# Two data-dependent blurs: inverse squares one row further ahead, and another split of the images between VectorE and GpSimd

## The chip, the cores and the metric

The program runs on one core of a Trainium2 chip. The metric is the device time in microseconds of one execution, lower is better. TensorE does the matrix products and transposes, VectorE (DVE), ScalarE (ACT) and GpSimd (POOL) the elementwise work, and SyncE (SP) starts transfers. Each engine works through its own instructions in the order in which the program lists them, and waits on semaphores for the others.

## What is computed

Eight images of 16 channels and 64 x 64 pixels pass through four layers, all in float32: L0 (a normalisation, depthwise convolutions and attention), L1 (a blur), L2 (a binary 3 x 3 convolution) and L3 (a blur again, with other weights). The change touches only the two blurs. Cut to what matters, a blur is:

```python
h = relu(einsum('bchw,co->bohw', x, w1) + b1)              # 32 hidden channels
ks = relu(einsum('bohw,o->bhw', h, w2[:, 0]) + b2[0]) * 20.0 + 1.0
sigma = ks / 3.0                                           # one width for each pixel
logits = -gauss_kernel / (2.0 * sigma[..., None, None] ** 2)   # 9 x 9 taps
wgt = exp(logits)
wgt = wgt / sum(wgt, axis=(-2, -1))
# low_freq = sum over the 81 taps of shifted x times wgt
enhanced = x + low_freq
out = (enhanced - mean) / sqrt(var + 1e-05)                # over h, w of each channel
```

The exponent of a tap is thus a fixed number (-4.5 times a squared distance) times 1/ks^2 of the pixel. This text calls these 1/ks^2 the inverse squares.

## The kernel before, in words

`blur` treats the picture in RB = 8 rows of blocks (r = 0 to 7), each of 8 pixel rows for all eight images. For a row r:

- **Inverse squares.** TensorE computes the hidden layer (`pe_hidden`, L921) and the sum over it (`pe_ks`, L930); ScalarE applies the activation between the two (`act_hidden`, L1040). VectorE adds the bias and clips (`dve_relu`, L1091), ScalarE squares (`act_square`, L1048), VectorE takes the reciprocal into `srow` (`dve_inverse`, L1099). From `srow` there are two ways. For the images that VectorE multiplies, TensorE turns it (`pe_ks_turn`, L937), VectorE copies it to `scl` (`dve_scale`, L1105), and TensorE spreads it over the partitions into one of four PSUM banks, four transposes for an image (`pe_spread`, L960). For the images that GpSimd multiplies, SyncE writes `srow` to DRAM (L1241) and reads it back broadcast to all partitions as `s_wide` (L1247).
- **Exponents.** VectorE multiplies the exponents by the inverse squares of an image (`dve_logit`, L1115), GpSimd does the same for its images (`pool_logit`, L1202). ScalarE takes the exponential of two images (a pair) at a time (`act_weight`, L1067). Pair k holds images 2k and 2k+1. The weights are in `wgt[r % 2]`.
- **Pixels.** GpSimd stages the row's pixels (`pool_stage`, L1190), TensorE transposes them (`pe_xt`, L945), ScalarE copies them to `xt` (`act_xt`, L1055).
- **Blur.** TensorE multiplies weights and pixels (`pe_blur`, L974), for images 0 to 3 (i = 0) and 4 to 7 (i = 1), each in two parts. VectorE copies each half's sum out of the one bank O_BANK (`dve_num`, L1123). TensorE turns it (`pe_turn`, L988), VectorE divides by the sum of the weights (`dve_mix`, L1129 and L1133), TensorE turns it back (`pe_low`, L996), and VectorE adds it to the picture and takes statistics (`dve_enhance`, L1141, `dve_stats`, L1145).

The work of several rows is interleaved, and the order on each engine is written out by hand in `pe_row`, `act_row`, `dve_row` and `pool_row`. In the pass of row r, TensorE ends row r-1's images 4 to 7, blurs row r's images 0 to 3, spreads row r+1 and computes the hidden layer of row r+2; VectorE prepares row r+1's inverse squares while it multiplies row r. `rows_of` writes out rows 0 and 1 and 6 to 8, and runs rows 2 to 5 in a hardware loop of two turns. Row 0 has all eight images on VectorE. Waits are on counts: `small` counts relu, reciprocal and scale, three a row; `logit` the images of VectorE; `logit_p` those of GpSimd; `weight` the exponentials; `blurred` the half blurs.

VectorE's order in a middle row of the kernel before, as `dve_row` has it: relu(r+1), image 0 of row r, inverse(r+1), image 1, scale(r+1), mix and num of row r-1, images 2 and 3 of its four, mix(r-1), num(r, 0), enhance(r-1), stats(r-1). The names of its four images are 0, 1, 4 and 5. ScalarE's order: square(r+1), the exponentials of pair 1 (GpSimd's images 2, 3), pair 0, the xt copy of row r+1, pair 3 (GpSimd's 6, 7), the hidden activations of row r+2, pair 2.

Of the kernel before, what the change touches and what calls it, by code (L numbers as in the profile page):

```python
# [836 lines left out]
def blur(nc, sem_, sb, tag, later, ident, vec, ps, pad, norm, to_clear, out, beside=None):  # L837
# [62 lines left out]
    def is0(r):  # L900
        return isinstance(r, int) and r == 0

    def slots(r):

        return list(enumerate(range(B) if is0(r) else BY_DVE))

    def by_slot(r, v):

        return v + 1 if is0(r) else 4 * r + 5 + v
# [148 lines left out]
    def act_weight(act, r, s, pair):  # L1058

        if is0(r):  # L1060
            act.wait_ge(logit, 2 * pair + 2)
        elif pair % 2 == 0:
            act.wait_ge(logit, by_slot(r, pair + 1))
        else:
            act.wait_ge(logit_p, 4 * r + pair - 5 + 2)
# [3 lines left out]
    def act_row(act, r, s, do):  # L1069
        if do.next and not do.first:  # L1070
            act_square(act, r + 1)
        if do.main:
            act_weight(act, r, s, 0 if do.first else 1)
        if do.next and do.first:
            act_square(act, r + 1)
        if do.main:
            act_weight(act, r, s, 1 if do.first else 0)
            act_xt(act, r + 1, 1 - s)
            act_weight(act, r, s, 2 if do.first else 3)
        if do.after_next:  # L1080
            act_hidden(act, r + 2)
        if do.main:
            act_weight(act, r, s, 3 if do.first else 2)
# [527 lines left out]
```

## Time and profile before

| | us |
|---|---|
| median of 3 runs | 533.4 |
| lowest and highest of them | 532.68, 534.13 |
| the profiled execution's own time | 531.34 |
| its span, first to last instruction | 529.4 |
| busy in the span: TensorE, VectorE, ScalarE, GpSimd | 412.6, 339.3, 260.6, 187.9 |
| the first blur lies at | 214 to 346 |
| the second blur lies at | 388.3 to 529.4 |
| mean granted TensorE clock, as a share of the full one | 0.927 |

The profile is one execution. Times in its rows are microseconds from the start of the span; L974 is line 974 of the kernel. PE is TensorE's matrix work and PEld its weight loads, which overlap. PEclk is the granted clock as a share of the full 2.4 GHz. In a timeline, a row may stand for several instructions of one kind (x8); the bracket at its end gives how long the engine was idle before it and who ended that. A row's duration can reach up to 0.1 us into the next one's start, since instructions of one engine overlap a little at their ends.

### The profile page before, as it was taken

How to read it: one execution, taken by the hardware profiler on the slowest of the kernel's cores; microseconds unless marked ns; L12 is line 12 of the kernel's file. 1: busy time of each engine (PE TensorE's matmuls, PEld its weight loads, DVE VectorE, ACT ScalarE, POOL GpSimd, SP SyncE). 2: the span in 40 equal slices, each digit the busy share in tenths (PEclk: the TensorE clock that was granted, in tenths of full speed). 3: DMA queues.
4: the chain of work that ended last, by engine and by line, in shares of the span. 5: the costliest groups of instructions: out<-in, count | busy, mean ns of one | idle time of the engine just before them, and what ended most of it. 6: DMA issues, size and time to landing. Idle time of an engine off the chain costs nothing. (4 is left out here: it accounts for less than half of the span.)

```text
span 529.4 us, 16123 instructions
## 1 busy us (share of the span) xinstructions
PE 412.6 (78%) x7024; PEld 293.8 (56%) x7024; DVE 339.3 (64%) x525; ACT 260.6 (49%) x284; POOL 187.9 (35%) x132
## 2 busy tenths in 40 slices
PE   4588998877999469668888888579956888788780
PEld 2277942225988412436666667457734666566660
DVE  2694587753888964554666668539534576566863
ACT  0664476663333000147767776511015577677771
POOL 3320013220000000307777777500030567867740
PEclk9968999996999869789999999979988899999986
DMA  8830000000000000002222223000000222222203
GB/s 190 194 136 1 2 1 0 1 0 1 4 2 1 3 0 0 1 6 79 83 84 81 80 82 84 2 1 1 0 1 0 83 85 83 84 80 80 83 4 158
DMA packets 17046, 24.67 MB, mean 47 GB/s; under 512 B 6736, under 2 KB 8545, under 8 KB 16865
## 3 DMA queue, kind: packets, MB, share of 16 engines
q1 hardware_dynamic: 15968, 23.52, 15.0%
q8 instruction: 43, 0.70, 0.5%
q10 hardware_dynamic: 1024, 0.36, 0.4%
q14 instruction: 11, 0.08, 0.0%
HBM read 21.53 MB, written 2.34 MB: 45 GB/s over the span
## 5 line engine op out<-in xcount | busy, mean ns | idle before, releaser
L1202 POOL TENSOR_TENSOR g_wgt<-g_exponents,g_s_wide 128x1024 f32<-128x1024 f32 x56 | 131.4, 2382 | 67.9 <-DMA g_s_wide<-g_s_rows 67.9
L1067 ACT ACTIVATE g_wgt<-g_wgt 128x2048 f32<-128x2048 f32 x64 | 121.6, 1909 | 17.2 <-DVE g_wgt L1115 11.0
L974 PE MATMUL ps<-g_wgt,g_xt 128*32 128x64 f32 x4096 | 72.5, 222 | 29.2 <-ACT g_wgt L1067 13.1
L974 PEld LDWEIGHTS ps<-g_wgt,g_xt 128*32 128x32 f32 x4096 | 62.0, 111 | 49.3 <-issue 36.9
L1115 DVE TENSOR_TENSOR g_wgt<-g_exponents,ps 128x1024 f32<-128x1024 f32 x72 | 84.6, 1202 | 2.6 <-PE ps L960 2.6
L1123 DVE COPY g_num<-ps 128x512 f32<-128x512 f32 x32 | 22.0, 687 | 64.0 <-PE ps L974 63.9
L1040 ACT ACTIVATE g_hid<-ps,vec 128x512 f32<-128x512 f32 x32 | 20.2, 683 | 84.0 <-PE ps L921 84.0
L960 PE MATMUL ps<-ident,g_scl 128*128 128x128 f32 x288 | 46.8, 302 | 4.9 <-DVE g_wgt L1115 2.6
L960 PEld LDWEIGHTS ps<-ident,g_scl 128*128 128x128 f32 x288 | 34.7, 150 | 10.4 <-DVE g_wgt L1115 4.2
L469 PE MATMUL ps<-conv_img,projblk 128*32 128x512 f32 x256 | 35.8, 679 | 0.0
L1412 PE MATMUL ps<-high,wb 128*128 128x512 f32 x72 | 30.3, 421 | 5.3 <-DVE rest L1441 5.3
L1190 POOL COPY g_tile<-pad_a 128x512 f32<-128x512 f32 (+1 forms) x18 | 10.6, 620 | 60.9 <-POOLq L732 53.4
L1055 ACT COPY g_xt<-ps 128x1024 f32<-128x1024 f32 x18 | 18.2, 1010 | 27.8 <-PE ps L945 27.8
L1190 POOL COPY g_tile<-pad_b 128x512 f32<-128x512 f32 (+1 forms) x18 | 10.6, 626 | 58.7 <-POOLq L1401 50.6
L526 ACT ACTIVATE biased<-ps,beta_o 128x512 f32<-128x512 f32 x32 | 24.0, 771 | 13.2 <-PE ps L469 13.2
L1412 PE MATMUL ps<-rest,wb 128*128 128x512 f32 x72 | 30.0, 416 | 0.0
L666 ACT ACTIVATE e<-ps 128x512 f32<-128x512 f32 x16 | 9.6, 597 | 33.0 <-PE ps L628 33.0
L787 PE MATMUL ps<-xrow,outblk 128*64 128x512 f32 x32 | 16.2, 1086 | 11.9 <-DVE xcol L827 11.9
L469 PEld LDWEIGHTS ps<-conv_img,projblk 128*32 128x32 f32 x256 | 12.5, 112 | 20.6 <-issue 16.1
L945 PE MATMUL ps<-ident,g_tile 128*128 128x128 f32 x144 | 22.1, 304 | 0.0
L988 PE MATMUL ps<-ident,g_num 128*128 128x128 f32 x128 | 20.3, 281 | 1.9 <-DVE g_num L1123 1.9
L617 PE MATMUL ps<-ident,rnh 128*128 128x128 f32 x128 | 19.1, 297 | 2.3 <-POOL rnh L709 2.3
(165 smaller groups left out, 718.0 us busy)
## 6 DMA issues: line engine op xcount, KB each, us to landing
g_s_wide<-g_s_rows SPq DMA_DIRECT2D x56, 256.0 KB, 3.8
x<-in_x SPq DMA_DIRECT2D x8, 256.0 KB, 6.8
x<-in_x SPq DMA_DIRECT2D x1, 2048.0 KB, 8.4
out<-g_result SPq DMA_DIRECT2D x4, 512.0 KB, 3.9
windows<-band SPq DMA_DIRECT2D x4, 256.0 KB, 5.1
g_s_rows<-g_srow SPq DMA_DIRECT2D x56, 4.0 KB
c_weight<-in_c_weight SPq DMA_DIRECT2D x1, 576.0 KB, 3.9
g_w<-in_g_w SPq DMA_DIRECT2D x2, 128.0 KB, 2.7
```

Source lines behind the costliest of these rows:

```text
L469: mm = pe.matmul(ps[q:q + 32, j % 4, :], projblk[:, 64 * cp + 32 * late:64 * cp + 32 * late + 32], lines(t, inner, strip, side), start=Tru ...
L526: act.activation(biased[:, j % 4, :], ps[:, j % 4, :], ACT.Identity, bias=beta[:, t:t + 1], scale=1.0).then_inc(proj_biased, 1)
L945: tr = pe.transpose(ps[:, bank, P * (cb % 4):P * (cb % 4) + P], tile[s][:, cb].rearrange("p r c -> p (r c)"), ident[:])
L960: tr = pe.transpose(ps[:, v % 4, P * k:P * k + P], spread(scl[s][:, k, b:b + 1], [P, P]), ident[:])
L974: mm = pe.matmul(ps[32 * j:32 * j + 32, O_BANK, 64 * cb:64 * cb + 64], xt[(s + t) % 2][:, cb, b, :], weights_of(s, b)[:, t, cb, :], start= ...
L988: tr = pe.transpose(ps[:, NT_BANK, P * k:P * k + P], num[i][:, P * k:P * k + P], ident[:])
L1067: act.activation(w, w, ACT.Exp).then_inc(weight, 1)
L1115: dve.tensor_tensor(weights_of(s, b), spread(gband[:].unsqueeze(2), shape), spread(s_in_ps, shape), ALU.mult).then_inc(logit, 1)
L1123: dve.tensor_copy(num[i][:], ps[:, O_BANK, :]).then_inc(num_out, 1)
L1190: ins = pool.tensor_copy(tile[s][:].rearrange("p (k o) r c -> p o k r c", o=2)[:, odd], cols.rearrange("p r (k c) -> p k r c", c=QC))
L1202: pool.tensor_tensor(weights_of(s, b), spread(gband[:].unsqueeze(2), shape), spread(s_wide[s][j][:].unsqueeze(1), shape), ALU.mult).then_i ...
L1412: mm = pe.matmul(ps[:, g % 4, :], wb[:, t, :], part[:, ROWS * g + dh:ROWS * g + dh + ROWS, dw:dw + W], start=(k == 0), stop=(k == 2 * TAPS ...
```

## The change

- Inverse squares are prepared for row r+2 in the pass of row r (relu, square, reciprocal, turn, scale, and SyncE's two transfers with them), where it was row r+1; the hidden layer and its sum for row r+3, where it was r+2. `scl` gets a third buffer. The place of these instructions among their neighbours in `pe_row` and `dve_row` stays.
- GpSimd multiplies images 3, 6 and 7 of a row, VectorE images 0, 1, 2, 4 and 5. TensorE spreads five images of a row, the fifth in the row's own pass, between the turn and the second part of the half blur. The banks now go by a running number (`nth`).
- ScalarE takes the exponentials in the order of pairs 0, 1, 2, 3, with the xt copy behind pair 1. Pair 1 now has one image of each engine.
- Half of the staging of pixels from row 2 on moves from GpSimd to ScalarE (`act_stage`, counted by `staged_a`), behind the xt copy.
- Rows 2 to 5 are written out, without the hardware loop. Row 0's pass has a function of its own for each engine, in which the inverse squares of rows 1 and 2 and the hidden layers of rows 2 and 3 are computed.

```diff
-    scl = [sb(f"scl{s}", [P, 4, B]) for s in range(2)]
+    scl = [sb(f"scl{s}", [P, 4, B]) for s in range(3)]
...
-    BY_DVE, BY_POOL = (0, 1, 4, 5), (2, 3, 6, 7)
+    BY_DVE, BY_POOL = (0, 1, 2, 4, 5), (3, 6, 7)
...
+    def image(r, v):
+        return v if r == 0 else BY_DVE[v]
+    def nth(r, v):
+        return v if r == 0 else B + len(BY_DVE) * (r - 1) + v
...
-        pe.wait_ge(small, 3 * RB if isinstance(g, int) and g == RB else 3 * g + 3)
+        if g >= 2:
+            pe.wait_ge(staged_a, g - 1)
+        pe.wait_ge(small, 3 * g + 3 if g < 2 else min(3 * g + 6, 3 * RB))
...
+    def pe_first_row(pe):
+        pe_spread(pe, 0, 0, 4)
+        pe_spread(pe, 0, 0, 5)
+        pe_ks_turn(pe, 1, 1)
+        pe_spread(pe, 0, 0, 6)
+        pe_spread(pe, 0, 0, 7)
+        pe_xt(pe, 1, 1)
+        pe_hidden(pe, 2)
+        pe_ks(pe, 2)
+        pe_spread(pe, 1, 1, 0)
+        pe_spread(pe, 1, 1, 1)
+        pe_ks_turn(pe, 2, 0)
+        pe_blur(pe, 0, 0, 0, 0)
+        pe_spread(pe, 1, 1, 2)
+        pe_hidden(pe, 3)
+        pe_blur(pe, 0, 0, 0, 1)
+        pe_spread(pe, 1, 1, 3)
+        pe_ks(pe, 3)
+    def pe_row(pe, r, s):
+        pe_blur(pe, r - 1, 1 - s, 1, 0)
+        pe_turn(pe, r - 1, 0)
+        if r + 2 < RB:
+            pe_ks_turn(pe, r + 2, s)
+        if r < RB:
+            pe_spread(pe, r, s, 4)
+        pe_blur(pe, r - 1, 1 - s, 1, 1)
+        if r + 1 < RB:
             pe_spread(pe, r + 1, 1 - s, 0)
             pe_spread(pe, r + 1, 1 - s, 1)
-        if do.main:
+        if r < RB:
             pe_xt(pe, r + 1, 1 - s)
-        if do.lag:
-            pe_turn(pe, r - 1, 1)
-        if do.main:
+        pe_turn(pe, r - 1, 1)
+        if r < RB:
             pe_blur(pe, r, s, 0, 0)
-        if do.next:
+        if r + 1 < RB:
             pe_spread(pe, r + 1, 1 - s, 2)
-        if do.after_next:
-            pe_hidden(pe, r + 2)
-        if do.main:
+        if r + 3 < RB:
+            pe_hidden(pe, r + 3)
+        if r < RB:
             pe_blur(pe, r, s, 0, 1)
-        if do.lag:
-            pe_low(pe, r - 1)
-        if do.next:
+        pe_low(pe, r - 1)
+        if r + 1 < RB:
             pe_spread(pe, r + 1, 1 - s, 3)
-        if do.after_next:
-            pe_ks(pe, r + 2)
+        if r + 3 < RB:
+            pe_ks(pe, r + 3)
...
+    def act_stage(act, g, s):
+        act.wait_ge(xt_mm, g - 1)
+        act.copy(*half_tile(g, s, 1)).then_inc(staged_a, 1)
+    def act_first_row(act):
+        act_weight(act, 0, 0, 0)
+        act_square(act, 1)
+        act_weight(act, 0, 0, 1)
+        act_xt(act, 1, 1)
+        act_stage(act, 2, 0)
+        act_hidden(act, 2)
+        act_square(act, 2)
+        act_weight(act, 0, 0, 2)
+        act_hidden(act, 3)
+        act_weight(act, 0, 0, 3)
+    def act_row(act, r, s):
+        if r + 2 < RB:
+            act_square(act, r + 2)
+        act_weight(act, r, s, 0)
+        act_weight(act, r, s, 1)
+        act_xt(act, r + 1, 1 - s)
+        if r + 2 <= RB:
+            act_stage(act, r + 2, s)
+        act_weight(act, r, s, 2)
+        if r + 3 < RB:
+            act_hidden(act, r + 3)
+        act_weight(act, r, s, 3)
...
+    def dve_first_row(dve):
+        dve_logit(dve, 0, 0, 0)
+        dve_logit(dve, 0, 0, 1)
+        dve_relu(dve, 1)
+        dve_logit(dve, 0, 0, 2)
+        dve_inverse(dve, 1, 1)
+        dve_logit(dve, 0, 0, 3)
+        dve_scale(dve, 1, 1)
+        dve_logit(dve, 0, 0, 4)
+        dve_relu(dve, 2)
+        dve_logit(dve, 0, 0, 5)
+        dve_inverse(dve, 2, 0)
+        dve_logit(dve, 0, 0, 6)
+        dve_scale(dve, 2, 0)
+        dve_logit(dve, 0, 0, 7)
+        dve_num(dve, 0, 0)
+    def dve_row(dve, r, s):
+        if r + 2 < RB:
+            dve_relu(dve, r + 2)
+        if r < RB:
             dve_logit(dve, r, s, 0)
-        if do.next:
-            dve_inverse(dve, r + 1, 1 - s)
-        if do.main:
+        if r + 2 < RB:
+            dve_inverse(dve, r + 2, s)
+        if r < RB:
             dve_logit(dve, r, s, 1)
-        if do.next:
-            dve_scale(dve, r + 1, 1 - s)
+        if r + 2 < RB:
+            dve_scale(dve, r + 2, s)
+        if r < RB:
+            dve_logit(dve, r, s, 2)
         dve_mix(dve, r - 1, 0)
         dve_num(dve, r - 1, 1)
-        if do.main:
-            dve_logit(dve, r, s, 2)
+        if r < RB:
             dve_logit(dve, r, s, 3)
+            dve_logit(dve, r, s, 4)
         dve_mix(dve, r - 1, 1)
...
+    def half_tile(g, s, odd):
+        cols = pad[:, BLK * g:BLK * g + BLK, BLK * odd:BLK * odd + W]
+        return (tile[s][:].rearrange("p (k o) r c -> p o k r c", o=2)[:, odd],
+                cols.rearrange("p r (k c) -> p k r c", c=QC))
     def pool_stage(pool, g, s):
-        if not (isinstance(g, int) and g < 2):
+        if g >= 2:
             pool.wait_ge(xt_mm, g - 1)
-        for odd in range(2):
-            cols = pad[:, bass.ds(BLK * g, BLK), BLK * odd:BLK * odd + W]
-            ins = pool.tensor_copy(tile[s][:].rearrange("p (k o) r c -> p o k r c", o=2)[:, odd],
-                                   cols.rearrange("p r (k c) -> p k r c", c=QC))
-        ins.then_inc(staged, 1)
+        else:
+            pool.tensor_copy(*half_tile(g, s, 1))
+        pool.tensor_copy(*half_tile(g, s, 0)).then_inc(staged, 1)
...
+    def pool_row(pool, r, s):
+        for j in range(len(BY_POOL)):
+            pool_logit(pool, r, s, j)
+        if r + 2 <= RB:
             pool_stage(pool, r + 2, s)
...
-    def rows_of(eng, row):
-        for r in range(2):
-            row(eng, r, r, Row(r))
-        with eng.Fori(0, 2) as i:
-            for p in range(2):
-                row(eng, 2 * i + 2 + p, p, Row(2))
-        for r in range(RB - 2, RB + 1):
-            row(eng, r, r % 2, Row(r))
...
-            rows_of(pool, pool_row)
+            pool_stage(pool, 2, 0)
+            for r in range(1, RB):
+                pool_row(pool, r, r % 2)
```

## Rows read from the trace of the kernel before

**Rows 1.** Windows: us, busy us (x instructions) by engine, PEclk, DMA share, GB/s
```profile
245.51:257.96 12.45, 10.77 (x310) 8.35 (x310) 8.24 (x13) 9.89 (x9) 8.66 (x7) 1.00 0.29 88
257.96:299.49 41.53, 34.51 (x941) 26.49 (x942) 28.52 (x45) 30.11 (x25) 31.81 (x19) 1.00 0.28 79
299.49:313.15 13.66, 11.41 (x315) 8.78 (x314) 9.46 (x16) 10.01 (x9) 10.51 (x7) 1.00 0.27 79
313.15:324.77 11.62, 9.59 (x310) 8.04 (x309) 9.45 (x15) 9.92 (x8) 8.44 (x6) 1.00 0.34 90
324.77:339.92 15.15, 10.88 (x416) 9.00 (x416) 10.93 (x17) 10.36 (x7) 12.92 (x5) 1.00 0.03 7
...
432.64:475.02 42.38, 34.50 (x941) 26.48 (x941) 28.38 (x45) 30.09 (x25) 32.17 (x20) 1.00 0.24 78
...
500.31:516.16 15.85, 12.51 (x416) 10.50 (x415) 11.13 (x18) 10.34 (x7) 8.32 (x4) 0.89 0.02 4
```

**Rows 2.** Timeline of VectorE: start us, us, engine, line, operation, [idle before, releaser]
```profile
324.77 0.69 DVE L1123 COPY g_num<-ps 128x512 f32<-128x512 f32 x1 [1.96 <-PE ps L974]
...
326.71 2.34 DVE L1115 TENSOR_TENSOR g_wgt<-g_exponents,ps 128x1024 f32<-128x1024 f32 x2
...
446.15 0.69 DVE L1123 COPY g_num<-ps 128x512 f32<-128x512 f32 x1 [3.98 <-PE ps L974]
...
448.49 1.21 DVE L1115 TENSOR_TENSOR g_wgt<-g_exponents,ps 128x1024 f32<-128x1024 f32 x1
```

**Rows 3.** Timeline of ScalarE, block 7 of the first blur, block 3 of the second
```profile
328.70 3.71 ACT L1067 ACTIVATE g_wgt<-g_wgt 128x2048 f32<-128x2048 f32 x2 [3.19 <-POOL g_wgt L1202]
332.31 0.99 ACT L1055 COPY g_xt<-ps 128x1024 f32<-128x1024 f32 x1
...
448.91 1.90 ACT L1067 ACTIVATE g_wgt<-g_wgt 128x2048 f32<-128x2048 f32 x1
451.67 1.91 ACT L1067 ACTIVATE g_wgt<-g_wgt 128x2048 f32<-128x2048 f32 x1 [0.86 <-DVE g_wgt L1115]
453.98 1.01 ACT L1055 COPY g_xt<-ps 128x1024 f32<-128x1024 f32 x1 [0.39 <-PE ps L945]
```

**Rows 4.** Timeline of TensorE in block 3 of the second blur
```profile
450.61 0.33 PE L937 MATMUL ps<-ident,g_srow 128*128 128x128 f32 x1 [0.73 <-DVE g_srow L1099]
...
455.23 1.10 PE L974 MATMUL ps<-g_wgt,g_xt 128*32 128x64 f32 x64 [0.93 <-ACT g_xt L1055]
456.26 0.65 PE L960 MATMUL ps<-ident,g_scl 128*128 128x128 f32 x4
456.75 1.88 PE L921 MATMUL ps<-pad_b,g_w 128*128 x4
```

**Rows 5.** Waits, whole span: us in total, times, longest us
```profile
POOL g_wgt L1202 <- DMA g_s_wide<-g_s_rows: 67.9, 14, 13.8
```

**Rows 6.** Timelines of row 0 in both blurs, then one window of it
```profile
233.70 0.94 DVE L1099 RECIPROCAL g_srow<-g_ks_sq 128x128 f32<-128x128 f32 x1
...
241.01 1.10 PE L974 MATMUL ps<-g_wgt,g_xt 128*32 128x64 f32 x64 [1.19 <-ACT g_xt L1055]
...
401.74 1.98 PE L921 MATMUL ps<-pad_b,g_w 128*128 128x512 f32 x4 [1.10 <-ACT g_xt L1055]
...
405.79 0.35 DVE L1091 TENSOR_SCALAR g_relu<-ps,vec 128x128 f32<-128x128 f32 x1 [6.94 <-PE ps L930]
...
408.57 0.95 DVE L1099 RECIPROCAL g_srow<-g_ks_sq 128x128 f32<-128x128 f32 x1 [0.17 <-ACT g_ks_sq L1048]
...
410.76 2.24 PE L960 MATMUL ps<-ident,g_scl 128*128 128x128 f32 x8 [0.84 <-DVE g_scl L1105]
...
412.80 1.70 PE L945 MATMUL ps<-ident,g_tile 128*128 128x128 f32 x8
...
409.50:412.80 3.30, 2.36 (x10) 1.77 (x11) 3.30 (x5) 0.85 (x1) 0.00 (x0) 0.69 0.03 8
```

More of the change, by code:

```diff
@@ L900, in is0 @@
     def is0(r):
[L901 to L909, printed above, removed]
+        return r == 0
+    def image(r, v):
+        return v if r == 0 else BY_DVE[v]
+    def nth(r, v):
+        return v if r == 0 else B + len(BY_DVE) * (r - 1) + v
     def weights_of(s, b):
@@ L915, in pe_hidden @@
     def pe_hidden(pe, r):
-        if not is0(r):
+        if r == 1 or r == 2:
             pe.wait_ge(xt_out, r)
-        rows = bass.ds(BLK * r + R, BLK)
+        elif r > 2:
+            pe.wait_ge(xt_out, r - 1)
+            pe.wait_ge(small, 3 * r)
+        rows = slice(BLK * r + R, BLK * r + R + BLK)
         for i, bank in enumerate((MLP_BANK, XT_BANK)):
@@ L1058, in act_weight @@
     def act_weight(act, r, s, pair):
[L1060 to L1065, printed above, removed]
+        on_dve = [v for v in range(B if r == 0 else len(BY_DVE)) if image(r, v) // 2 == pair]
+        on_pool = [j for j, b in enumerate(BY_POOL) if r > 0 and b // 2 == pair]
+        if on_dve:
+            act.wait_ge(logit, nth(r, on_dve[-1]) + 1)
+        if on_pool:
+            act.wait_ge(logit_p, len(BY_POOL) * (r - 1) + on_pool[-1] + 1)
         w = wgt[s][pair][:].rearrange("p b t k m -> p (b t k m)")
         act.activation(w, w, ACT.Exp).then_inc(weight, 1)
-    def act_row(act, r, s, do):
-        if do.next and not do.first:
-            act_square(act, r + 1)
-        if do.main:
-            act_weight(act, r, s, 0 if do.first else 1)
-        if do.next and do.first:
-            act_square(act, r + 1)
-        if do.main:
[L1077 to L1083, printed above, removed]
+    def act_stage(act, g, s):
[24 more added lines that the diff above has]
+        act_weight(act, r, s, 3)
     def dve_relu(dve, r):
@@ L1096, in dve_inverse @@
         dve.wait_ge(ks_squared, r + 1)
-        if not (isinstance(r, int) and r < 3):
+        if not (r < 3):
             dve.wait_ge(s_stored, 64 * (r - 2))
@@ L1203, in pool_logit @@
                            spread(s_wide[s][j][:].unsqueeze(1), shape), ALU.mult).then_inc(logit_p, 1)
-    def pool_row(pool, r, s, do):
-        if do.main and not do.first:
-            for j in range(len(BY_POOL)):
-                pool_logit(pool, r, s, j)
-        if do.next:
-            pool_stage(pool, r + 2, s)
-    class Row:
-        def __init__(self, r):
-            self.first, self.main, self.lag = r == 0, r < RB, 0 < r <= RB
-            self.next, self.after_next = r + 1 < RB, r + 2 < RB
-    def rows_of(eng, row):
-        for r in range(2):
-            row(eng, r, r, Row(r))
-        with eng.Fori(0, 2) as i:
-            for p in range(2):
-                row(eng, 2 * i + 2 + p, p, Row(2))
-        for r in range(RB - 2, RB + 1):
-            row(eng, r, r % 2, Row(r))
+    def pool_row(pool, r, s):
+        for j in range(len(BY_POOL)):
+            pool_logit(pool, r, s, j)
+        if r + 2 <= RB:
+            pool_stage(pool, r + 2, s)
     def quarter(j):
@@ L1281, in _ @@
             pe.wait_ge(const_ready, 4)
-            rows_of(pe, pe_row)
+            pe_first_row(pe)
+            for r in range(1, RB + 1):
+                pe_row(pe, r, r % 2)
         @block.scalar
@@ L1290, in _ @@
             act_hidden(act, 1)
-            rows_of(act, act_row)
+            act_first_row(act)
+            for r in range(1, RB):
+                act_row(act, r, r % 2)
             act.wait_ge(tail, 2)
@@ L1316, in _ @@
             dve.wait_ge(band_ready, 2)
-            rows_of(dve, dve_row)
+            dve_first_row(dve)
+            for r in range(1, RB + 1):
+                dve_row(dve, r, r % 2)
             dve.wait_ge(stat, RB)
```

69 lines of the change are left out of this document (18 added, 51 removed).

## Prediction

> **What bounds the kernel now.** I read the windows of the two blurs first. The change touches only these; they fill 214 to 346 and 388 to 529 us of the span. A window here runs from one start of the copy at L1123 to the next, that is from one image row block r to the following one. I call this start num(r). In both blurs a middle block lasts 13.66 us, the first 12.45, the sixth 11.6; the last stretch holds the block of row 7 and the remainder up to the second copy [rows 1]. No engine fills a middle block: TensorE is busy 11.4 of 13.66, VectorE 9.5, ScalarE 10.0, GpSimd 10.5. So a chain through several engines sets it, and its links count, not the sums.
>
> The timelines give the links. From num(2) at 446.15 VectorE runs copy, enhance, statistics, relu, the first image of the next block (448.49), the reciprocal of the inverse squares, and the second image [rows 2]. That second image releases the exponential of pair 0 at 451.67, 5.52 us after num. ScalarE has by then done the exponential of pair 1, GpSimd's pair, at 448.91, in time that it would otherwise idle away. Then it idles 0.86 and, after pair 0, 0.39 us, the latter for TensorE's staging transposes, and copies xt at 453.98 [rows 3]. TensorE waits for that copy (0.93) and runs half blur, spread, hidden layer, half blur; their end is the next num [rows 4]. TensorE's own arm of the loop (turn at 450.61, which waits 0.73 for the reciprocal, half blur, two spreads, transposes) reaches xt at the same time as ScalarE's arm, to 0.4 us. GpSimd is a side arm: it waits 67.9 us in all for the broadcast rows, 14 times, but its result is late only where ScalarE shows a wait on it, in row 7 of a blur (3.19 us in the first) [rows 5, 3].
>
> **The change, part by part.**
>
> *Order of pairs.* In the new row order ScalarE does square, exp of pair 0, exp of pair 1, xt copy. The exp of pair 0 still needs the second image of the row, which in VectorE's order still stands behind num, enhance, statistics, relu, image 0 and the reciprocal; only the index of relu and reciprocal has grown. So pair 0 starts as late as before, and pair 1 can't fill the wait, because it is behind it. Two exponentials back to back put the xt copy 3.61 us after the first one's start (328.70 to 332.31), where it was 2.31 us (451.67 to 453.98) [rows 3]. **+1.30 us for each block**, on the path.
>
> *One more spread and image.* VectorE gets a fifth image, GpSimd loses one. An image costs VectorE 1.17 us (two in 2.34) [rows 2]. In VectorE's order image 2 falls behind image 1, which is released already; it ends near num+6.6, image 4 near num+10.2. Cover: VectorE idles 3.98 us ahead of num and pair 2's exponential starts near num+10.5. Zero on the path; without the cover 1.2 a block. TensorE gets four transposes, between the turn and the half blur: 0.55 us, the size of one spread (0.49 in steps, 0.65 as shown) [rows 4]. Its arm then reaches the end of the xt transposes near num+8.2 (7.7 before), while ScalarE is now free only at num+9.0. So this spread is hidden behind the exponential; without this cover, 0.55 a block.
>
> *GpSimd.* Three images of 2.38 us and half a staging copy instead of four and a whole one. Its inputs come a row earlier, and its idle time grows. Off the path: worth nothing in middle blocks. In row 7 it ends the wait of 3.19 us, but there the exponentials now wait for VectorE's images: 324.77 to 326.71 is 1.94, two images 2.34, so they start at num+4.3 where GpSimd let them start at 328.70, num+3.9 [rows 2, 3].
>
> *ScalarE's half staging copy.* No such copy exists there; between 0.5 us (half the xt copy, which is twice as large and takes 1.01 [rows 3]) and 1.0; I take 0.6. It stands behind the xt copy, which is the last thing of ScalarE that TensorE waits for, and ScalarE is idle for 3.6 of 13.66 us. Zero.
>
> *Loops unrolled.* Between num and image 0 the unrolled row needs 1.94 us where the loop row needs 2.34, with a relu of 0.26 (0.35 as shown, 0.09 under the next): 0.14 saved. Blocks 5 and 6 differ by 2.04, the hidden layer is 1.81 of it (1.88 as shown); the other 0.23 is what the loop costs elsewhere [rows 1, 2, 4, 6]. **−0.37 in blocks 2 to 5.** One gap of 1.3 us in the second blur's loop, which TensorE spends on issue, makes its blocks 2 to 4 last 42.38, not 41.53; I take it to be gone.
>
> *The first row.* Before, VectorE ran images 0 to 7 of row 0 with one relu and reciprocal between. Now it has relu(2) between images 4 and 5. relu(2) waits for a whole chain: image 3 (now behind reciprocal(1)), spread 7, transposes, xt copy, hidden(2), activation, ks(2). Images 5, 6, 7 are queued behind that wait, and so are the exponentials of pairs 2 and 3 and the second reciprocal; TensorE has this turn ahead of its first half blur. From reciprocal(1) on, by the second blur: reciprocal and image 0.95 + 1.17, spread 1.12 (two in 2.24), transposes 1.70, xt copy 1.01, hidden to relu 4.05 (401.74 to 405.79), relu and image 0.35 + 1.17, reciprocal 0.95, turn 0.3, less some 0.2 by which they overlap: 12.6 us to the first half blur. Before it was 415.69 − 408.57 = 7.12. **+5.4.** In the first blur the reciprocal can start one image (1.17) earlier than its 233.70, and the old way took 241.01 − 233.70 = 7.31: 12.6 − 1.17 − 7.31 = **+4.1** [rows 6]. From the half blur to num(0) the work is the same, 4.5 us (241.01 to 245.51).
>
> The clock enters here. The granted clock was 0.69 from 409.5 to 412.8, after TensorE had waited several times, and 1.00 in all middle blocks; eight spread transposes took 2.24, where four take 0.65 in a middle block [rows 6, 1, 4]. The new first row leaves TensorE with more waits, so I take the slow values. The Trainium skill (TensorE: Matmul & The Clock Gate, "What's actually happening") says that the full clock is released by activity and the default is half of it; by it a head that stays at full clock would be some 1.1 us shorter in each blur (0.5 in the spread, 0.6 in the transposes), 2.2 in all. The trace agrees so far as these rows go.
>
> **The sum.** New blocks: row 1 has no loop, and its xt copy waits as the others do: 12.45 + 1.3 = 13.75. Rows 2 to 4: 13.66 + 1.30 − 0.37 = 14.6 each. Row 5 loses the hidden layer: 14.6 − 1.88 = 12.7. Row 6 has neither relu nor reciprocal: first exponential at num+4.3, xt 3.61 later, and from there 3.9 to the next num (11.62 − 5.38 − 2.31): 11.8. Row 7 and the remainder: xt at num+7.95, and from xt to the second copy 339.92 − 332.31 = 7.6: 15.55. Together 13.75 + 43.8 + 12.7 + 11.8 + 15.55 = 97.6. Before: first blur 12.45 + 41.53 + 13.66 + 11.62 + 15.15 = 94.4; second 12.45 + 42.38 + 13.66 + 11.63 + 15.85 = 96.0 (its blocks 1, 5 and 6 agree with the first's to 0.01) [rows 1]. So +3.2 and +1.6, and the heads +4.1 and +5.4: **+14.3 us**. The profiled execution took 531.34 us with a span of 529.4 and lies 2.1 below the median of 533.4. On the median: **548 us**, 2.8% slower.
>
> **Rivals.**
> 1. *Only TensorE's arm counts.* The exponential of pair 1 would not push xt, or my 1.30 is given back by another link. For it: the two arms were only 0.4 us apart. Against it: ScalarE's order is fixed. Then a block grows by 0.55 and not 1.30, 0.75 less in 14 blocks, 10.5 us less: 537. Chance 0.08.
> 2. *Faster: the reciprocal's place was the bound.* If taking it a row ahead truly takes TensorE's turn off the row's loop, each block gives back the 0.73 wait, 12 blocks, the loop costs 0.37 in 8, and GpSimd's lateness about 3 in each row 7: 8.8 + 3.0 + 6 = 18 less, against heads of 9.5: 525. It decides from the point where a block is shorter than about 13.0. Against it: relu, reciprocal and turn keep their places between the same neighbours in all three queues. Chance 0.06.
> 3. *The clock drops in the rows.* TensorE now idles 2 to 3 us a block in pieces; if the granted clock fell as in the heads, five spreads at 0.9 or more instead of 0.55 and the rest alike would add some 3 us a block, on 14 blocks 42 on top: 590. Nothing shows a fall in middle blocks, where idle pieces of 0.9 us are already borne at 1.00. Part of it, in the heads and row 7 (0.89 in the last stretch [rows 1]), is more likely and adds 2 to 5: up to 553. Chance of the first 0.03.
> 4. *The change does nothing that can be told:* its losses meet gains of the same size, within 0.3%, which is 1.6 us and about what a measurement of this kernel can tell from no change: 533. Chance 0.03.
>
> **How the numbers follow.** My forecast has 0.80, with its own range of 543 to 553 (heads 1.5 either way each, staging and spread up to 0.2 a block). The range for 8 in 10 takes in rival 1 below and the clock's part above: 537 to 554. Faster holds rival 2 and a remainder, 0.08; same 0.03; slower 0.89.
>
> **What would show it.** In the new profile: middle blocks of 14.6 us at clock 1.00; two exponentials back to back ahead of each xt copy, ScalarE idle 2.5 us ahead of them; no ScalarE wait on GpSimd, and GpSimd below 60% in the blurs; TensorE's wait for xt near 1.7 us; in the first row a wait of some 6 us of VectorE at relu for TensorE. Blocks under 13.7 or a first row as short as before would prove me wrong.

## The result, and the profile after

The changed kernel takes 552.6 us, median of 4 runs (551.83 to 554.7); the kernel of before took 533.07 beside it, median of 4. The ratio is 1.0369, with a 95% interval of 1.0337 to 1.0402: 19.5 us slower. The forecast was 548, with a range of 537 to 554. The profiled execution has a span of 550.1 us against 529.4. Here and below a median is over all runs of a kernel, while a ratio is over the undisturbed runs of both kernels of one session, so that quotients of medians differ a little from the ratios.

The windows of the changed kernel, cut as those of [rows 1] at the starts of the first copy of a row (blocks 1, 2 to 4, 5, 6, and 7 with the remainder; the second blur's blocks 1, 5 and 6 read 13.82, 12.85 and 11.79):

```profile
248.22:262.04 13.82, 11.34 (x314) 8.71 (x314) 9.38 (x15) 10.30 (x10) 7.64 (x4) 1.00 0.30 83
262.04:305.85 43.81, 36.04 (x952) 27.57 (x952) 31.69 (x49) 31.23 (x28) 22.93 (x12) 1.00 0.18 58
305.85:320.16 14.31, 10.48 (x314) 8.56 (x314) 10.56 (x16) 11.14 (x9) 7.65 (x4) 1.00 0.21 59
320.16:331.95 11.79, 9.58 (x297) 8.01 (x298) 9.40 (x13) 7.49 (x6) 9.18 (x4) 1.00 0.02 4
331.95:347.42 15.47, 11.31 (x420) 9.28 (x420) 12.07 (x18) 10.87 (x7) 2.29 (x1) 1.00 0.01 3
...
449.75:493.49 43.74, 35.94 (x952) 27.46 (x952) 31.69 (x49) 31.24 (x28) 22.94 (x12) 1.00 0.19 58
...
518.13:536.80 18.67, 14.52 (x420) 11.63 (x420) 12.16 (x18) 10.86 (x7) 0.00 (x0) 0.82 0.01 3
```

A middle block now lasts 14.6 us (43.81 and 43.74 for three) where it took 13.66. All of them have a granted clock of 1.00, so nothing here comes from a slower TensorE. The last stretch of the second blur has 0.82. The same links as in [rows 2 to 4], in block 3 of the second blur, first on VectorE:

```profile
449.75 0.69 DVE L1155 COPY g_num<-ps 128x512 f32<-128x512 f32 x1 [3.91 <-PE ps L977]
...
451.93 1.21 DVE L1147 TENSOR_TENSOR g_wgt<-g_exponents,ps 128x1024 f32<-128x1024 f32 x1
453.06 0.94 DVE L1131 RECIPROCAL g_srow<-g_ks_sq 128x128 f32<-128x128 f32 x1
453.92 1.16 DVE L1147 TENSOR_TENSOR g_wgt<-g_exponents,ps 128x1024 f32<-128x1024 f32 x1
...
455.09 1.21 DVE L1147 TENSOR_TENSOR g_wgt<-g_exponents,ps 128x1024 f32<-128x1024 f32 x1
```

then on ScalarE:

```profile
455.11 3.73 ACT L1085 ACTIVATE g_wgt<-g_wgt 128x2048 f32<-128x2048 f32 x2 [2.67 <-DVE g_wgt L1147]
458.75 0.98 ACT L1073 COPY g_xt<-ps 128x1024 f32<-128x1024 f32 x1
459.64 0.61 ACT L1090 COPY g_tile<-pad_b 128x512 f32<-128x512 f32 x1
```

and on TensorE (turn, the fifth image's spread, first half blur):

```profile
454.06 0.33 PE L941 MATMUL ps<-ident,g_srow 128*128 128x128 f32 x1 [0.56 <-DVE g_srow L1131]
454.22 0.60 PE L963 MATMUL ps<-ident,g_scl 128*128 128x128 f32 x4
...
459.83 1.10 PE L977 MATMUL ps<-g_wgt,g_xt 128*32 128x64 f32 x64 [1.51 <-ACT g_wgt L1085]
```

From num at 449.75 the exponential of pair 0 starts 5.36 us later (5.52 before, with the loop). Image 2 on VectorE starts at 455.09, the exponential of pair 1 follows that of pair 0 at once (3.73 for both), and the xt copy comes 3.64 us after the start of the first; in [rows 3] it was 2.31. TensorE waits 1.51 us for it, where it waited 0.93 [rows 4]. (The bracket names the exponential, but that had ended at 458.84; the matmuls wait for both and start 0.1 us after the copy's end.) ScalarE idles 2.67 us ahead of the exponentials. Who waited for whom, over the whole span:

```profile
POOL g_wgt L1244 <- PE ps L977: 69.2, 22, 3.7
...
ACT g_wgt L1085 <- DVE g_wgt L1147: 45.3, 18, 4.5
...
DVE g_relu L1123 <- PE ps L934: 33.3, 8, 8.3
...
PE ps L977 <- ACT g_wgt L1085: 29.8, 28, 1.7
```

GpSimd no longer waits mainly for the broadcast rows [rows 5] but for the half blurs that free its weights: its inputs come early, and it is 27% busy where it was 35%. No wait of ScalarE for GpSimd is left. All that was bought is slack on an engine that wasn't setting the pace, but for its lateness in row 7. The new first row, one line of the first blur and then the second blur, with two windows of it:

```profile
240.13 0.35 DVE L1123 TENSOR_SCALAR g_relu<-ps,vec 128x128 f32<-128x128 f32 x1 [5.74 <-PE ps L934]
...
417.18 1.16 DVE L1147 TENSOR_TENSOR g_wgt<-g_exponents,ps 128x1024 f32<-128x1024 f32 x1
...
418.35 1.21 DVE L1147 TENSOR_TENSOR g_wgt<-g_exponents,ps 128x1024 f32<-128x1024 f32 x1
...
419.02 1.91 PE L951 MATMUL ps<-ident,g_tile 128*128 128x128 f32 x8
...
422.04 3.71 PE L925 MATMUL ps<-pad_b,g_w 128*128 128x512 f32 x4 [1.10 <-ACT g_xt L1073]
...
427.82 0.35 DVE L1123 TENSOR_SCALAR g_relu<-ps,vec 128x128 f32<-128x128 f32 x1 [8.26 <-PE ps L934]
...
430.62 1.91 PE L977 MATMUL ps<-g_wgt,g_xt 128*32 128x64 f32 x64
...
418.50:421.00 2.50, 2.44 (x12) 2.04 (x12) 1.06 (x1) 1.81 (x2) 0.00 (x0) 0.54 0.09 32
422.00:425.80 3.80, 3.71 (x4) 1.17 (x4) 0.00 (x0) 0.52 (x2) 2.28 (x1) 0.53 0.43 130
```

VectorE waits 5.74 us for relu(2) in the first blur and 8.26 in the second. There TensorE works at half its clock (0.54 and 0.53, thus 1.2 GHz): the hidden layer takes 3.71 us where 1.98 and 1.88 are seen in [rows 6, 4], the half blur 1.91 instead of 1.10.

### The profile page after: what moved, and what is told of

Read it like the earlier page. It is cut to its first block and busy times, and to the rows that moved or that the text cites. A ratio compares the mean times of both kernels' runs of the same rounds, so it can differ in the third digit from the quotient of the medians.

```text
span 550.1 us, 15973 instructions
## 1 busy us (share of the span) xinstructions
PE 422.2 (77%) x7080; PEld 299.3 (54%) x7080; DVE 356.2 (65%) x539; ACT 267.2 (49%) x298; POOL 148.7 (27%) x104
## 5 line engine op out<-in xcount | busy, mean ns | idle before, releaser
L1085 ACT ACTIVATE g_wgt<-g_wgt 128x2048 f32<-128x2048 f32 x64 | 120.1, 1907 | 45.3 <-DVE g_wgt L1147 45.3
L1244 POOL TENSOR_TENSOR g_wgt<-g_exponents,g_s_wide 128x1024 f32<-128x1024 f32 x42 | 99.1, 2376 | 105.7 <-PE ps L977 69.2
L1147 DVE TENSOR_TENSOR g_wgt<-g_exponents,ps 128x1024 f32<-128x1024 f32 x86 | 101.5, 1204 | 2.6 <-PE ps L963 2.6
L977 PE MATMUL ps<-g_wgt,g_xt 128*32 128x64 f32 x4096 | 74.6, 226 | 32.4 <-ACT g_wgt L1085 29.8
L977 PEld LDWEIGHTS ps<-g_wgt,g_xt 128*32 128x32 f32 x4096 | 63.9, 114 | 51.4 <-ACT g_wgt L1085 36.4
L963 PE MATMUL ps<-ident,g_scl 128*128 128x128 f32 x344 | 56.8, 298 | 4.4 <-DVE g_wgt L1147 3.9
L963 PEld LDWEIGHTS ps<-ident,g_scl 128*128 128x128 f32 x344 | 40.5, 147 | 12.5 <-DVE g_wgt L1147 7.9
L1123 DVE TENSOR_SCALAR g_relu<-ps,vec 128x128 f32<-128x128 f32 x16 | 5.5, 342 | 33.3 <-PE ps L934 33.3
L1073 ACT COPY g_xt<-ps 128x1024 f32<-128x1024 f32 x18 | 17.9, 994 | 14.8 <-PE ps L951 14.8
L925 PE MATMUL ps<-pad_b,g_w 128*128 128x512 f32 x32 | 17.1, 660 | 4.1 <-ACT g_xt L1073 2.2
```

Of the source, the lines that this page charges most:

```text
L963: tr = pe.transpose(ps[:, nth(r, v) % 4, P * k:P * k + P], spread(scl[r % 3][:, k, b:b + 1], [P, P]), ident[:])
L977: mm = pe.matmul(ps[32 * j:32 * j + 32, O_BANK, 64 * cb:64 * cb + 64], xt[(s + t) % 2][:, cb, b, :], weights_of(s, b)[:, t, cb, :], start= ...
L1085: act.activation(w, w, ACT.Exp).then_inc(weight, 1)
L1147: dve.tensor_tensor(weights_of(s, b), spread(gband[:].unsqueeze(2), shape), spread(s_in_ps, shape), ALU.mult).then_inc(logit, 1)
L1244: pool.tensor_tensor(weights_of(s, b), spread(gband[:].unsqueeze(2), shape), spread(s_wide[s][j][:].unsqueeze(1), shape), ALU.mult).then_i ...
```

## The experiments

All ratios are to the kernel of before, run beside each on the same chip. The blocks are the seven stretches from num(r) to num(r+1) of a blur; "middle block" gives the length of one without a gap in the first blur, "first row" the time from the first relu to the first num in the first and second blur. A "gap" is idle time of TensorE inside a run of matmuls that the profile puts down to issue, since it shows nothing that the engine waited for.

```
kernel                 median us  ratio (95%)              first row     middle block
before                 533.07     1                        27.5, 27.5    13.66
changed                552.6      1.0369 (1.0337, 1.0402)  31.3, 35.5    14.58
e1_split               540.9      1.0126 (1.0055, 1.0197)  31.9, 32.6    13.78
e2_split_spread        542.44     1.0167 (1.0104, 1.0231)  33.0, 32.6    13.78
e3_before_natural      561.16     1.0527 (1.0460, 1.0593)  27.2, 28.9    15.0, 16.5
e4_before_unrolled     531.66     0.9977 (0.9941, 1.0014)  27.5, 27.6    13.21
e5_one_ahead           531.8      1.0014 (0.9968, 1.0060)  27.4, 27.7    13.78
e6_ahead_alone         537.0      1.0087 (1.0054, 1.0119)  31.8, 35.5    13.21
e7_late_turn           533.59     0.9989 (0.9954, 1.0023)  33.0, 33.7    12.87
e8_late_turn_head      532.17     0.9998 (0.9958, 1.0038)  25.9, 26.9    12.86
e9_xt_first            529.14     0.9928 (0.9898, 0.9959)  23.5, 23.6    13.3
e10_xt_first_unrolled  527.53     0.9925 (0.9891, 0.9960)  25.9, 26.0    12.95
e11_split_natural      552.23     1.0383 (1.0321, 1.0445)  30.6, 35.5    14.57
e12_warm               542.96     1.0204 (1.0149, 1.0259)  30.6, 33.0    14.58
```

### The order of the exponentials

e1, from the changed kernel:

```diff
-    BY_DVE, BY_POOL = (0, 1, 2, 4, 5), (3, 6, 7)
+    BY_DVE, BY_POOL = (0, 1, 4, 5, 7), (2, 3, 6)
     # act_row
-        act_weight(act, r, s, 0)
         act_weight(act, r, s, 1)
+        act_weight(act, r, s, 0)
```

> The changed kernel with GpSimd on images 2, 3, 6 (VectorE 0, 1, 4, 5, 7) and the exponential of pair 1 ahead of pair 0 again. Theory (natural order puts one exponential on the path, 1.30 us a block): that exponential goes back into ScalarE's wait; then TensorE's arm sets the xt copy (near num+8.2), so middle blocks go from 14.58 to 13.8 and the last two lose about 0.95: 541 us. Rival (the exponential is all there is, TensorE's extra spread costs nothing even now): 13.3 a block, 535. Rival (order of pairs costs nothing, the extra VectorE image or the unrolled code does): 552 as before this edit.

e11 has the first of these two edits alone.

> The changed kernel with the other split alone (GpSimd 2, 3, 6, VectorE 0, 1, 4, 5, 7), exponentials in natural order. It parts the two edits of e1. Theory (the order puts the exponential on the path, whoever multiplies the images): blocks of 14.6 and about 552, 3.7% over the kernel of before. Rival (it was image 2 on VectorE that held pair 1 back): blocks of 13.8, near e1's 1.3%.

e3 is the same question asked of the kernel of before:

```diff
     # act_row, rows from 1 on
-            act_weight(act, r, s, 1)
             act_weight(act, r, s, 0)
+            act_weight(act, r, s, 1)
             act_xt(act, r + 1, 1 - s)
```

> The kernel of before with one edit: the exponential of pair 0 ahead of pair 1, ahead of the xt copy. Theory: +1.30 us in blocks 1 to 6 and +0.4 in block 7 of both blurs, 16 us more: 549.5; middle blocks 14.96. Rival (TensorE's arm sets the block, so the order is hidden): 533, blocks 13.66.

e1 takes 2.4% off the changed kernel's ratio, 13 us of the 19.5, and its blocks are 13.78; e11, with the same split but the natural order, stays at 14.57 and 3.8%. So it is the order, not who multiplies image 2. (In the changed kernel the two go together: with image 2 on VectorE, ready only after image 1, pair 1 can't come first.) Not all of the 13 us is the order, though. The profiles' blocks with the remainder are 4.2 and 6.2 us shorter in e1, and the second blur's first row is 2.9 shorter, although its code is the same in both: its hidden layer took 1.98 us in e1 and 3.71 in the changed kernel. That part is TensorE's clock. ScalarE in block 2 of e1's second blur:

```profile
445.54 1.90 ACT L1085 ACTIVATE g_wgt<-g_wgt 128x2048 f32<-128x2048 f32 x1
448.30 1.91 ACT L1085 ACTIVATE g_wgt<-g_wgt 128x2048 f32<-128x2048 f32 x1 [0.86 <-DVE g_wgt L1147]
451.10 1.01 ACT L1073 COPY g_xt<-ps 128x1024 f32<-128x1024 f32 x1 [0.89 <-PE ps L951]
```

Pair 1's exponential stands ahead, and the xt copy starts 2.8 us after pair 0's and no longer 3.64; the 0.89 idle ahead of it says that TensorE's arm sets it now. e3 went further than the forecast: +5.3% and not +3.1%. Block 4 with 15.0 us is what was expected, but others last 16.5. TensorE and the xt copy in one of these, and its window beside that of block 4:

```profile
268.04 0.99 ACT L1055 COPY g_xt<-ps 128x1024 f32<-128x1024 f32 x1
...
269.27 1.33 PE L974 MATMUL ps<-g_wgt,g_xt 128*32 128x64 f32 x64 [2.22 <-ACT g_xt L1055]
...
270.54 1.11 PE L960 MATMUL ps<-ident,g_scl 128*128 128x128 f32 x4
...
271.45 2.86 PE L921 MATMUL ps<-pad_a,g_w 128*128 x4
...
259.06:275.49 16.43, 13.12 (x315) 9.85 (x315) 9.43 (x15) 9.97 (x9) 10.32 (x7) 0.90 0.24 68
292.20:307.20 15.00, 11.40 (x316) 8.77 (x315) 9.52 (x16) 9.88 (x10) 8.77 (x6) 1.00 0.25 72
```

The granted clock is 0.90 in the long block and 1.00 in the other. TensorE had waited 2.22 us for the xt copy, and then the spread took 1.11, the hidden layer 2.86, the half blur 1.33 (0.65, 1.88 and 1.10 in [rows 4]). This is my third rival, at work in some blocks of a kernel where the wait is 2.22 and not in the changed one, where it is 1.51; its price is 1.5 us a block, half of what I gave it. Block 4 has the same wait of 2.22 and the full clock, and it idled longer ahead of the turn (0.69 against 0.39), so the wait alone doesn't decide it, and no limit is read from this.

### TensorE's arm, the fifth spread and the loop

e2, from e1:

```diff
     # pe_row
+        if r < RB:
+            pe_spread(pe, r, s, 4)
         if r + 2 < RB:
             pe_ks_turn(pe, r + 2, s)
-        if r < RB:
-            pe_spread(pe, r, s, 4)
```

> As e1, and TensorE spreads the fifth image ahead of the turn of the inverse squares, where it waits for the reciprocal anyway. Theory: the 0.55 us of the spread leaves the arm, blocks 13.3, about 5 us less than e1: 536. Rival (the spread was already covered in e1): same as e1.

> The kernel of before with rows 2 to 5 written out. Theory: 0.37 us less in each of 8 blocks: 530, blocks 13.3. Rival (loop overhead is hidden, or the longer code costs more instruction fetch): 533 or above.

e5, from e4, in short (all waits recounted):

```diff
-    BY_DVE, BY_POOL = (0, 1, 4, 5), (2, 3, 6, 7)
+    BY_DVE, BY_POOL = (0, 1, 4, 5, 7), (2, 3, 6)
     # five spreads and images a row; pairs 1, 0, xt, 2, hidden, 3
```

> Rows written out, inverse squares only one row ahead and the old first row, GpSimd on three images (2, 3, 6), the exponential of pair 1 ahead of pair 0. Against e1 this undoes the second row of look-ahead. Theory: the first row is as long as before (27.5 us from the first relu to the first copy, not 32), but the rows 5 to 7 get their old length back, since the hidden layer and the reciprocal are in them again; blocks stay at 13.8 by the fifth spread: 533. Rival (the long first row is a pure loss of some 5 us a blur): 10 us under e1, 531 or less, with rows 5 to 7 as short as in e1.

e2 brought nothing; my theory for it was wrong. TensorE in a block of e2:

```profile
451.90 0.65 PE L963 MATMUL ps<-ident,g_scl 128*128 128x128 f32 x4
452.91 0.65 PE L963 MATMUL ps<-ident,g_scl 128*128 128x128 f32 x4 [0.36 <-DVE g_wgt L1147]
```

The second spread of the next row waits 0.36 us for VectorE. The bank that it writes is free only when image 4 (VectorE's third) is multiplied. With four images to a row it was free after the second, since the four banks go round. So there is a third arm, as long as TensorE's own.

In e4 the blocks fell about as forecast (13.21, by 0.45 for 0.37), but the time by only 0.2%, which is no difference. The profile puts 13.8 us of TensorE's idle time ahead of L974 down to issue, where the kernel of before has 6.3, but 8.5 of these are 12 waits of 0.71 like this one:

```profile
263.55 1.01 ACT L1055 COPY g_xt<-ps 128x1024 f32<-128x1024 f32 x1 [0.31 <-PE ps L945]
...
264.66 1.10 PE L974 MATMUL ps<-g_wgt,g_xt 128*32 128x64 f32 x64 [0.71 <-issue]
```

The matmuls start 0.1 us after the xt copy ends, as in every one of the 12: this is the known wait for xt under another name. True gaps, in the middle of a half blur, add up to 5.2 us in e4, the longest 3.2, and to 3.5 in the kernel of before (2.8 of its 6.3 are waits for xt); 1.9 more lie among e4's transposes. That is 3.6 us more than before, as much as eight shorter blocks save. Block 6 of the first blur, with the gap of 3.2, lasts 14.9 instead of 11.6.

e5 comes to 531.8 us, near both forecasts, but its rows are the theory's: the first row is 4.5 to 4.9 us shorter than e1's in each blur, and blocks 5 to 7 are longer again, 37.5 us in the first blur where e1 has 34.9, although a gap of 2.3 us lies in these.

### The look-ahead alone, and put to use

e6, from the changed kernel, in short:

```diff
-    BY_DVE, BY_POOL = (0, 1, 2, 4, 5), (3, 6, 7)
+    BY_DVE, BY_POOL = (0, 1, 4, 5), (2, 3, 6, 7)
     # four spreads and images a row; pairs 1, 0, xt, 3, hidden, 2
```

> The look-ahead alone: two rows ahead with the new first row, rows written out, half the staging on ScalarE, but GpSimd on its four images, four spreads, and the exponentials in the old order. Theory: middle blocks of 13.2 as in the unrolled kernel of before, first row 32 us, rows 5 to 7 shorter by the work that is already done and by GpSimd's wait: 527 to 531. Rival (the first row's loss is not returned): 539.

e7, from e6:

```diff
     # pe_row
-        if r + 2 < RB:
-            pe_ks_turn(pe, r + 2, s)
         pe_blur(pe, r - 1, 1 - s, 1, 1)
         if r + 1 < RB:
             pe_spread(pe, r + 1, 1 - s, 0)
-            pe_spread(pe, r + 1, 1 - s, 1)
+        if r + 2 < RB:
+            pe_ks_turn(pe, r + 2, s)
         if r < RB:
             pe_xt(pe, r + 1, 1 - s)
+        if r + 1 < RB:
+            pe_spread(pe, r + 1, 1 - s, 1)
     # dve_row
-        if r + 2 < RB:
-            dve_inverse(dve, r + 2, s)
         if r < RB:
             dve_logit(dve, r, s, 1)
+        if r + 2 < RB:
+            dve_inverse(dve, r + 2, s)
```

> e6 with the look-ahead put to use: VectorE takes the second image ahead of the reciprocal, and TensorE turns the inverse squares only after the half blur and one spread. Theory (the reciprocal's place between num and the second image is what the row waits for): exponential of pair 0 at num+4.5 and not 5.4, xt at num+6.9, blocks of 12.5: 520. Rival (TensorE's own work sets the row by now, 11.2 us and its waits): blocks of 13.0 or more, 526 or above.

> e7 with a first row in which VectorE multiplies all eight images and copies the first sum before relu(2), and a second row that holds the second preparation. Theory (the first row is long because images 5 to 7 stand behind relu(2)): first row about 25.5 us, block 1 about 15.5, together 3 us less than e7 in each blur: 514. Rival (the chain of the preparations is serial wherever it stands): as e7.

The look-ahead alone costs 0.9% over the kernel of before (4.6 us), between the two theories: middle blocks are 13.2, the first row 31.8 and 35.5, and what the last rows give back is partly eaten by gaps (7.8 us in its half blurs and 2.0 elsewhere; another 9.2 that the profile puts down to issue are waits for xt, as in e4).

e7 shows where the look-ahead would have a use: with the reciprocal behind the second image and the turn behind the half blur, a block falls to 12.87, 0.4 above my 12.5, since the scale copy (VectorE waits 0.42 for the turn) is late. But the first row takes 33 us, and the sum is that of before. e8's first row is short (25.9), its second 19.6 and 20.7 us: the rival holds, the second preparation is a serial chain and only moved.

### The best version

e9, from the kernel of before, with neither look-ahead nor another split:

```diff
     # pe_row
-        if do.next:
-            pe_ks_turn(pe, r + 1, 1 - s)
         if do.lag:
             pe_blur(pe, r - 1, 1 - s, 1, 1)
         if do.next:
-            pe_spread(pe, r + 1, 1 - s, 0)
-            pe_spread(pe, r + 1, 1 - s, 1)
+            pe_ks_turn(pe, r + 1, 1 - s)
         if do.main:
             pe_xt(pe, r + 1, 1 - s)
+        if do.next:
+            pe_spread(pe, r + 1, 1 - s, 0)
+            pe_spread(pe, r + 1, 1 - s, 1)
     # dve_row
-        if do.next:
-            dve_inverse(dve, r + 1, 1 - s)
         if do.main:
             dve_logit(dve, r, s, 1)
+        if do.next:
+            dve_inverse(dve, r + 1, 1 - s)
```

> The kernel of before (loop, one row ahead, four images on GpSimd, old order of pairs) with two places changed: VectorE takes the second image ahead of the reciprocal, and TensorE runs the second part of the half blur, then the turn, then the transposes of xt, and only then the two spreads. Theory (what a row waits for is the two arms between num and the xt copy, and both shorten without any look-ahead): blocks of about 13.1 in the loop, first row 2 us shorter since two spreads leave the way to the xt copy, block 7 up to 1 us longer because GpSimd gets its rows later: 524. Rival (the spreads only move behind xt and delay the half blur as much): 532, blocks of 13.6.

> e9 with rows 2 to 5 written out. Theory (0.4 us a block less, given back by the gaps that TensorE spends on issue): blocks of 12.8 to 12.9 where there is no gap, time within 2 us of e9. Rival (no cost of written-out rows): 3 us under e9.

Both beat both kernels: e9 529.14 us, 0.7% under the kernel of before, e10 527.53 (0.8% under), not to be told apart; the intervals of both ratios end below 1. TensorE in e9 does the transposes of xt straight behind the turn, and the spreads in the time in which ScalarE copies:

```profile
444.36 0.33 PE L937 MATMUL ps<-ident,g_srow 128*128 128x128 f32 x1
444.97 1.09 PE L945 MATMUL ps<-ident,g_tile 128*128 128x128 f32 x8 [0.28 <-DVE g_scl L1105]
445.90 1.04 PE L960 MATMUL ps<-ident,g_scl 128*128 128x128 f32 x8
```

The first row falls to 23.5 us in e9 and to 25.9 in e10, although its code is the same in both. The difference is TensorE's clock (windows over the xt transposes, two spreads and the half blur, e9 and then e10):

```profile
232.80:236.20 3.40, 3.03 (x81) 2.75 (x82) 3.30 (x3) 2.25 (x2) 0.00 (x0) 1.00 0.32 82
...
236.50:241.00 4.50, 4.48 (x80) 4.10 (x80) 3.26 (x3) 2.82 (x2) 0.00 (x0) 0.62 0.38 141
```

In the kernel of before the same transposes took 1.91 us at 237.90, so they too met the lower clock. Of the 4 us by which e9's first row is shorter, the order is thus worth about 1.6 (27.5 to 25.9, both at the lower clock; I had forecast 2) and the clock the rest. The gain is smaller than the 9 us expected. Blocks are 13.3 and not 13.1; in some, GpSimd now is late, as its rows start later (two exponentials, then xt, on ScalarE in block 5 of the first blur):

```profile
295.59 3.72 ACT L1067 ACTIVATE g_wgt<-g_wgt 128x2048 f32<-128x2048 f32 x2 [0.75 <-POOL g_wgt L1202]
299.40 1.01 ACT L1055 COPY g_xt<-ps 128x1024 f32<-128x1024 f32 x1
```

and gaps of 0.7 to 1.8 us remain. In the second blur, block 3 with two gaps has 15.9 and block 4 behind it 14.8, at a granted clock of 0.88. GpSimd's price in row 7 is larger than my 1 us: ScalarE waits 4.75 us for it in the first blur (3.19 before), and blocks 6 and 7 together last 24.5 us where they took 22.3. In e10 they last 24.5 too; its block 7 alone has 9.7, but a gap of 3.1 us of TensorE lies in its block 6, during which GpSimd went on.

### TensorE's clock in the first row

e12, from the changed kernel (the added transposes feed nothing):

```diff
     # pe_first_row
         pe_spread(pe, 0, 0, 5)
+        pe_idle_work(pe, 10)      # transposes of ident into NT_BANK
         pe_ks_turn(pe, 1, 1)
...
         pe_xt(pe, 1, 1)
+        pe_idle_work(pe, 8)
         pe_hidden(pe, 2)
+        pe_idle_work(pe, 8)
         pe_ks(pe, 2)
```

> The changed kernel with 26 transposes of a constant into an unused bank, put into three waits of TensorE in row 0 of each blur (ahead of the turn, of hidden(2) and of ks(2)); they add work and serve nothing else. Theory (TensorE's lower clock lengthens the first row): granted clock near 1.00 there, the spread, transposes, hidden layer and half blur at 0.65, 1.04, 1.88 and 1.10, first rows of 30.5 to 31.5 in both blurs, 2 to 4 us less than the changed kernel. Rival (the clock does not follow this work, or the added work delays as much as it gives): no change, first rows of 31.3 to 35.5.

Added work makes the kernel faster: 1.0204 and not 1.0369, 8.8 us between the ratios. Transposes of xt, added work, hidden layer, added work, half blur in the second blur, and two windows:

```profile
415.67 1.92 PE L951 MATMUL ps<-ident,g_tile 128*128 128x128 f32 x8
...
417.37 1.54 PE L1004 MATMUL ps<-ident 128*128 128x128 f32 x8
...
418.75 1.92 PE L925 MATMUL ps<-pad_b,g_w 128*128 128x512 f32 x4
...
420.50 1.04 PE L1004 MATMUL ps<-ident 128*128 128x128 f32 x8
...
425.39 1.10 PE L977 MATMUL ps<-g_wgt,g_xt 128*32 128x64 f32 x64
...
414.80:417.30 2.50, 2.45 (x12) 2.45 (x13) 1.22 (x2) 1.91 (x1) 0.00 (x0) 0.54 0.12 35
418.70:420.60 1.90, 1.90 (x7) 0.89 (x6) 0.00 (x0) 0.45 (x1) 0.00 (x0) 1.00 0.66 227
```

The clock is still 0.54 in the spread and xt transposes (1.92), but back at 1.00 for the hidden layer (1.92, was 3.71) and the half blur (1.10, was 1.91). The first rows are 0.65 and 2.5 us shorter, where I had expected 2 to 4 in each. (In the first blur most of it was at full clock already; the half blur there fell from 1.89 to 1.10.) That is 3.2 of the 7.8 us by which the two profiles' spans differ. The rest: the last stretch of the second blur has 15.46 us and not 18.67, 3.2 less; the start of the first blur comes 1.25 earlier, in code that is the same; a gap in block 5 of the first blur is absent (1.5), one in block 6 of the second is new (1.3). Why the clock holds in the last row when work is added in the first isn't shown. The Trainium skill (TensorE: Matmul & The Clock Gate, "Why this matters for your kernels") advises against idle gaps between bursts of matmuls. The trace points the same way: with work put into its waits, the granted clock of the hidden layer is 1.00 and not 0.53.

## Why the prediction was right, and where it was off

- **Order of pairs, +1.30 us a block.** Right: 3.64 us from exponential to xt for the forecast 3.61, blocks of 14.58 for 14.6; e1 and e11 show that the order is the cause, of 8 to 10 of the 19.5 us by the profiles' blocks (2.0 of the 10 are the second blur's last stretch, whose clock was 1.00 in e1 and 0.82 in the changed kernel). All of it could be read from the old trace: ScalarE can't fill a wait with work that is queued behind it.
- **Fifth spread and image, zero.** Right while the exponential covers them. e1 takes the cover away: the xt copy then starts at num+8.2, as forecast, blocks 13.78 against 13.21. But I named one arm and there are two: e2 shows that the bank's wait for VectorE's third image holds the same time.
- **GpSimd, worth nothing.** Right; 27% busy and no wait for it. Block 7 of the first blur went from 10.68 to 11.06 us, the 0.4 that I had given it.
- **Half staging copy, 0.6 us, zero.** Measured 0.61, ahead of pair 2, hidden: e6 has it and e4 hasn't, and both have blocks of 13.21.
- **Loop, −0.37 a block.** Right in the blocks (13.66 to 13.21 in e4), not in the time: 0.2% less, within its interval. Gaps took the place; what makes them stays open. In the half blurs they come to 3.5 us in the kernel of before and to 5.2, 6.3 and 7.8 in e4, e1 and e6, which are written out, yet to 2.5 in the changed kernel and 2.0 in e5, also written out.
- **First row, +4.1 and +5.4.** By the profile +3.8 and +8.0. The mechanism, images 5 to 7 behind relu(2) and its chain, is in the trace (waits of 5.74 and 8.26 for relu). The second blur's is mis-sized: I took the slow clock for spread and transposes only, and it lasted through the hidden layer and half blur, 1.7 and 0.8 us more; e12 gives these back. In e1 and e2 the same code took 32.6 us in the second blur, near my 32.9, and in e6 and e11 35.5. So this term is known only to some 3 us: its size depends on where the clock falls.
- **The blocks' sum, 97.6.** First blur 99.2, second 100.9. The first holds one gap of 1.2 us in block 5 (14.31 for 12.85); the second a last stretch of 18.67 for 15.55 at a clock of 0.82, with a gap of 0.98 in it. By the spans the change costs 20.7 us, 6.4 over the forecast of 14.3: +1.3 in the first blur, +5.9 in the second (first row 2.6, last stretch 3.1), −0.8 outside the blurs. The medians differ by 19.5. So 552.6 lies above my own 548 by about the clock's part, which I had only among the rivals (2 to 5 us, up to 553).
- **Rivals.** The first (TensorE's arm alone) is refuted by the blocks. The second (faster) too: the reciprocal did keep its place, and when e7 moves it, a block falls by a further 0.34 us under e4's. The third is half true: no fall in the middle blocks, but in first row and last; e3 has it in some middle blocks too, at 1.5 us each and not 3.

Additively: e4 to e6 is the look-ahead with its first row, 1.1% or 6 us; e4 to e5 the fifth spread, 0.4%, not clear of noise; the order 2.4%, with the clock's 2.9 us of the first row in it.

## What to carry to other kernels

Look-ahead pays only if the queue order uses it: here every preparation kept its neighbours, so the loop's chain stayed, while the first row paid for the longer lead. Before handing work to another engine, read which engine's queue holds the last link, and put what is ready early ahead of what is late. And ask of each wait made longer what TensorE's clock does in it.

## What the runs showed of the hardware that I had not expected

- 26 useless transposes in TensorE's waits in each blur came with a program 1.6% faster (1.0369 to 1.0204); the granted clock of a hidden layer went from 0.53 to 1.00 and its time from 3.71 to 1.92 us.
- In e3 a block's wait of 2.22 us came with a clock of 0.90 in some blocks and 1.00 in others of the same code, 16.5 against 15.0 us. In e9 and e10 one and the same first row took 23.5 and 25.9 us, by the clock.
- Straight runs of small matmuls have gaps of up to 3.2 us, at other places from one kernel to the next. With those in TensorE's other work they come to 3.6, 6.3 and 7.8 us more in e4, e6 and e7 than in the kernel of before; in e4 that is what the shorter blocks gave. Their cause was not tried.
